# Attention heads in 32-row tiles of TensorE instead of block-diagonal operands, in a transformer layer with a mixture of experts

## The chip, the core and the metric

The kernel runs on one core of one Trainium2 chip. The metric is the device time of one execution in microseconds (us), the lower the better. The engines are TensorE (PE in the profile, its weight loads PEld), VectorE (DVE), ScalarE (ACT), GpSimd (POOL) and SyncE (SP, which here only issues DMAs). Each runs its own instructions in program order and waits on semaphores.

## The reference

One decoder layer on 16 sequences of 128 tokens of width 128, with a context of 77 tokens a sequence. Attention has 16 heads of width 8; the mixture of experts has 8 experts, of which each token uses 2. All is float32.

```python
def _attn(q_in, k_in, v_in, wq, bq, ..., causal):
    Q = (q_in @ wq + bq).reshape(Bq, Sq, H, HD)      # Kp and V in the same way
    scores = jnp.einsum('bqhd,bkhd->bhqk', Q, Kp) / jnp.sqrt(jnp.float32(HD))
    if causal: scores = jnp.where(mask, scores, -jnp.inf)
    a = jax.nn.softmax(scores, axis=-1)
    return jnp.einsum('bhqk,bkhd->bqhd', a, V).reshape(Bq, Sq, Dm) @ wo + bo

x = _layernorm(x + _attn(x, x, x, *sa, True), ln1_g, ln1_b)
x = _layernorm(x + _attn(x, encoder_output, encoder_output, *ca, False), ln2_g, ln2_b)
x = _layernorm(x + _moe(x, router_w, router_b, e_w1, e_b1, e_w2, e_b2), ln3_g, ln3_b)
```

## The kernel before

**Stages.** The attention part works on pairs of sequences: 8 pairs, `p`, and within a pair the sequence `u` (0 or 1). Each pair passes through self attention (SA), cross attention (CA) and the router (RT). The list `ORDER` (line 267) is the order of the steps in one iteration, written out by hand; a row `(SA, "scores", 2, 0)` is step, kind, part and how many pairs ahead or behind the iteration's own. Every engine walks through the same list and does its share of each step, so three pairs are under way at once, and an engine never takes a later step before an earlier one. Steps with four parts (`scores`, `weights`, `mix`, `restore`) have part = 2u + half, two groups of heads each. `home` (line 285) gives each step its PSUM banks. After the pairs comes the expert stage (39 slots of 128 rows, lines 603 to 628 on TensorE), and a last layer norm over all tokens (lines 996 to 1027), called the tail.

**Precision.** Queries and keys are split into a high and a low part in the reduced format fp32r. `spread_terms` multiplies them with the 0/1 matrices `spread` so that each head has 32 rows: 8 rows for the shift, and three times 8 for the products high x high, high x low, low x high. Four heads j = 0..3 fill the 128 rows of a group g = 0..3; the result is `qu` (by ScalarE, line 663) and `ku` (by VectorE, line 790), which also adds ones (`kones`) in the eight shift rows.

**Scores.** To keep the four heads of a group apart in one matmul over 128 rows, one operand is block-diagonal. `km` (line 503) has `ku`'s rows of head j in column block j and zeros elsewhere. GpSimd zeroes `km` and `qm` once (lines 1032 and 1033), and for each pair SP copies 24 rows of each head from `ku` to `km` (line 366, four DMAs) and from `qu` to `qm` (line 372, four DMAs). The scores of a group are one matmul of 512 columns (4 x 78 in CA), after a bf16 matmul with the causal mask in SA (line 502). VectorE takes the negated row maxima (`nm`, line 807), splits them (`mm`, lines 815 and 817), TensorE transposes them (line 510), and ScalarE writes them into the eight shift rows of each head in `qm`, in four copies (line 674):

```python
for j in range(J):
    rows = slice(32 * j, 32 * j + 8)
    src = bank[home[k, "shift", u][0]][rows, 0:P].rearrange("r (o n) -> r o n", o=1).to_broadcast([8, GROUPS, P])
    act.copy(k.qm[rows, :, j, P * u:P * u + P], src).then_inc(k.s_sha, 1)
```

**Weights, values, restore.** `weights` computes the shifted, transposed scores again as `ku` x `qm` (line 522), ScalarE takes the exponential into `pt` (line 682), and in SA GpSimd zeroes what lies over the diagonal (line 1048). `mix` multiplies a group's `vo` (32 value columns and 32 columns of ones, line 535) with 512 columns of `pt`; two groups stand in one bank, in rows 0 to 63 and 64 to 127. ScalarE copies the bank to `us` (line 689), `restore` transposes it back in four pieces (line 546), and VectorE takes the reciprocals of the sums and multiplies the head's own 8 of 32 value columns (lines 829 and 833). `turn_heads` and `norm` finish the attention: output projection, residual, batch-norm statistics (line 847), and on GpSimd the epsilon added to the variance (line 1056) and the power -1/2 (line 1058). The tail does the same at lines 1089 and 1091.

**Setup.** VectorE clears and fills constants (lines 757 to 772), counted in `s_setup`; the first `spread_terms` on TensorE and all of VectorE's steps wait for all of it. GpSimd adds the output bias to `residual` (line 1038) when that is loaded.

## Time and profile before

| | |
|---|---|
| median of 3 runs | 504.39 us (501.17 to 506.9) |
| the profiled execution | 503.74 us |
| its span (first to last instruction) | 501.9 us, 8915 instructions |
| TensorE busy, weight loads | 370.7 us (74%), 245.4 us (49%) |
| VectorE busy | 314.4 us (63%) |
| ScalarE busy | 283.2 us (56%) |
| GpSimd busy | 185.5 us (37%) |

The profile is of one execution. Busy time is the time in which an engine has an instruction under way; TensorE's matmuls overlap, and their ends are modelled, so the distance between starts says more than a duration. Idle time before an instruction is put down to what released it. In the span the first 60 us are the filling of the pipeline of pairs, 60 to 322 us its steady run, to 385 us its emptying and the router's last steps, to 470 us the experts, and then the tail.

### The profile page before, as it was taken

How to read it: one execution, taken by the hardware profiler on the slowest of the kernel's cores; microseconds unless marked ns; L12 is line 12 of the kernel's file. 1: busy time of each engine (PE TensorE's matmuls, PEld its weight loads, DVE VectorE, ACT ScalarE, POOL GpSimd, SP SyncE). 2: the span in 40 equal slices, each digit the busy share in tenths (PEclk: the TensorE clock that was granted, in tenths of full speed). 3: DMA queues.
4: the chain of work that ended last, by engine and by line, in shares of the span. 5: the costliest groups of instructions: out<-in, count | busy, mean ns of one | idle time of the engine just before them, and what ended most of it. 6: DMA issues, size and time to landing. Idle time of an engine off the chain costs nothing.

```text
span 501.9 us, 8915 instructions
## 1 busy us (share of the span) xinstructions
PE 370.7 (74%) x2121; PEld 245.4 (49%) x2121; DVE 314.4 (63%) x1055; ACT 283.2 (56%) x648; POOL 185.5 (37%) x253
## 2 busy tenths in 40 slices
PE   2348668989989989989988988757504999999300
PEld 1313445465455465455465463343203999999300
DVE  9632555678778778778778777455371555555192
ACT  2017268669669669679679669526211455555132
POOL 9403211231441441441441442512220455555363
PEclk9998899999999999999999999975855999999855
DMA  7330301511341341341341341040871122222243
GB/s 209 91 73 0 71 20 43 150 40 26 83 127 31 80 130 30 80 128 30 82 128 30 82 130 24 23 136 13 260 186 48 39 66 66 59 61 51 61 114 84
DMA packets 47819, 39.92 MB, mean 80 GB/s; under 512 B 4762, under 2 KB 44559, under 8 KB 47768
## 3 DMA queue, kind: packets, MB, share of 16 engines
q1 hardware_dynamic: 45496, 35.11, 27.3%
q0 software_dynamic: 2272, 4.24, 2.6%
q8 instruction: 20, 0.33, 0.3%
q14 instruction: 31, 0.25, 0.2%
HBM read 13.66 MB, written 14.79 MB: 57 GB/s over the span
## 4 chain that ended last, share of the span: by engine, by line
PE 26%; DVE 24%; issue 11%; POOL 10%; DVEq 7%; SPq 6%; ACT 6%; DMA 5%; POOLq 0%; ACTq 0%
POOL dispatched L1073 5%; PE bank L535 4%; SPq L366 4%; PE bank L479 4%; DVEq L977 3%; PE bank L522 3%; PE bank L480 3%; ACT ca_qm L674 2%; DVE ca_us L980 2%; DVE yb L990 2%; DVE ca_nm L807 2%; SPq L372 2%; PE bank L503 2%; DMA sa_km<-sa_ku 2%; DMA sa_xin<-in_x 2%
## 5 line engine op out<-in xcount | busy, mean ns | idle before, releaser
L733 ACT ACTIVATE sa_us<-bank,expert_b 128x128 f32<-128x128 f32 x156 | 45.0, 368 | 49.9 <-PE bank L617 38.5
L1048 POOL TENSOR_SCALAR_AFFINE_SELECT sa_pt<-sa_pt 128x512 f32<-128x512 f32 x64 | 39.1, 639 | 70.8 <-ACT sa_pt L682 70.7
L1082 POOL DMA_INDIRECT results<-sa_us,xs x39 | 41.6, 1066 | 52.9 <-DVE sa_us L992 50.3
L807 DVE TENSOR_REDUCE sa_nm<-bank 128x4 f32<-128x512 f32 x64 | 41.5, 684 | 14.0 <-PE bank L503 13.8
L1073 POOL DMA_INDIRECT dispatched<-r_sent,r_row x32 | 32.0, 1001 | 43.8 <-DVE r_sent L933 36.5
L617 PE MATMUL bank<-xsT,ca_us 128*128 128x128 f32 x312 | 45.8, 292 | 3.1 <-DVE ca_us L980 1.6
L674 ACT CAST sa_qm<-bank 8x512 fp32r<-8x512 f32 x64 | 36.9, 577 | 14.0 <-PE bank L510 12.3
L617 PEld LDWEIGHTS bank<-xsT,ca_us 128*128 128x128 f32 x312 | 39.7, 199 | 7.8 <-issue 4.6
L628 PE MATMUL bank<-ca_pt,sa_us 128*128 x312 | 42.3, 279 | 0.2 <-issue 0.2
L674 ACT CAST ca_qm<-bank 8x512 fp32r<-8x512 f32 x64 | 36.8, 576 | 9.0 <-PE bank L510 7.8
L682 ACT ACTIVATE sa_pt<-bank 128x512 f32<-128x512 f32 x64 | 34.8, 596 | 9.4 <-PE bank L522 9.3
L628 PEld LDWEIGHTS bank<-ca_pt,sa_us 128*128 128x128 f32 x312 | 38.6, 195 | 0.4 <-issue 0.4
L682 ACT ACTIVATE ca_pt<-bank 77x512 f32<-77x512 f32 x64 | 33.7, 598 | 9.0 <-PE bank L522 9.0
L503 PE MATMUL bank<-sa_km,sa_qu 128*128 128x512 f32 x64 | 37.5, 640 | 0.0
L502 PE MATMUL bank<-causal_bf,ident_bf 128*128 128x512 bf16 x64 | 27.1, 423 | 13.6 <-DMA sa_km<-sa_ku 12.8
L535 PE MATMUL bank<-ca_pt,ca_vo 77*64 77x512 f32 x128 | 35.8, 632 | 0.1
L535 PE MATMUL bank<-sa_pt,sa_vo 128*64 128x512 f32 x128 | 35.8, 631 | 0.0
L1056 POOL TENSOR_SCALAR sa_ve<-sa_ba 128x1 f32<-128x1 f32 x16 | 6.1, 384 | 69.1 <-DVE sa_ba L851 69.1
L807 DVE TENSOR_REDUCE ca_nm<-bank 128x4 f32<-128x308 f32 x64 | 26.8, 472 | 7.7 <-PE bank L503 7.4
L689 ACT COPY ca_us<-bank 128x512 f32<-128x512 f32 x32 | 18.8, 586 | 17.5 <-PE bank L535 16.9
L522 PE MATMUL bank<-sa_qm,sa_ku 128*128 128x512 f32 x64 | 24.3, 456 | 4.8 <-ACT sa_qm L674 3.6
L980 DVE COPY ca_us<-sa_pt 128x512 f32 x39 | 16.7, 427 | 15.2 <-PE bank L617 12.2
(207 smaller groups left out, 863.4 us busy)
## 6 DMA issues: line engine op xcount, KB each, us to landing
dispatched<-filler SPq DMA_DIRECT2D x17, 520.0 KB, 4.5
sa_km<-sa_ku SPq DMA_DIRECT2D x32, 96.0 KB
sa_qm<-sa_qu SPq DMA_DIRECT2D x32, 96.0 KB
ca_qm<-ca_qu SPq DMA_DIRECT2D x32, 96.0 KB
xs<-dispatched SPq DMA_DIRECT2D x39, 65.0 KB
sa_pt<-in_e_w SPq DMA_DIRECT2D x8, 256.0 KB, 5.0
ca_pt<-in_e_w SPq DMA_DIRECT2D x8, 256.0 KB, 6.1
sa_pt<-results SPq DMA_DIRECT2D x8, 256.0 KB, 4.9
```

Source lines behind the costliest of these rows:

```text
L503: pe.matmul(dst, k.qu[:, g, P * u:P * u + P], k.km[:, g, :, k.keys * u:k.keys * u + k.kpad], start=not k.causal, stop=True).then_inc(k.s_s ...
L522: pe.matmul(bank[b][0:k.keys, :], k.ku[:, g, k.keys * u:k.keys * u + k.keys], k.qm[:, g, :, P * u:P * u + P], start=True, stop=True).then_ ...
L535: ins = pe.matmul(bank[b][64 * (g % 2):64 * (g % 2) + 64, :], k.vo[:, u, g, :], k.pt[u][:, 512 * g:512 * g + 512], start=True, stop=True)
L617: ins = pe.matmul(bank[2 * b + c // 2][:, P * (c % 2):P * (c % 2) + P], w1_now[b][:, P * c:P * c + P], xsT[b][:, :], start=True, stop=True)
L628: ins = pe.matmul(bank[4 + b][:, 0:D], hid[b][:, c, :], w2[:, bass.ds(expert, 1), c, :].rearrange("f o d -> f (o d)"), start=(c == 0), sto ...
L674: act.copy(k.qm[rows, :, j, P * u:P * u + P], src).then_inc(k.s_sha, 1)
L682: act.activation(k.pt[u][:, 512 * g:512 * g + 512], bank[home[k, "weights", u][g % 2]][0:k.keys, :], ACT.Exp, scale=SCALE).then_inc(k.s_ex, 1)
L733: act.activation(hid[b][:, c, :], bank[2 * b + c // 2][:, P * (c % 2):P * (c % 2) + P], ACT.Gelu, bias=b1[:, bass.ds(expert * FC + c, 1)]) ...
L807: dve.tensor_reduce(k.nm[:, u, g, :], bank[home[k, "scores", u][g % 2]][:, :].rearrange("q (j n) -> q j n", j=J)[:, :, 0:k.keys], AX.X, AL ...
L1048: pool.affine_select(out=blockg, in_=blockg, compare_op=ALU.is_ge, fill=0.0, base=0, pattern=[[0, J], [1, P]], channel_multiplier=-1).then ...
L1073: pool.indirect_dma_start(out=dispatched, out_offset=bass.IndirectOffsetOnAxis(ap=r.row[:, v, c:c + 1], axis=0), in_=r.sent[:, v, c, :], i ...
L1082: pool.indirect_dma_start(out=results, out_offset=bass.IndirectOffsetOnAxis(ap=xs[v][:, P:P + 1].bitcast(I32), axis=0), in_=ys[v], in_offs ...
```

## The change

The block-diagonal operands `km` and `qm` go, with their memsets on GpSimd, their sixteen DMAs a pair on SP and the four copies of the shift on ScalarE.

- `scores`: each matmul takes the 32 rows of one head j of one group g from `qu` and `ku` (128 columns, 78 in CA). A part now holds two heads j (for all four g) in place of two groups; the matmuls of the two heads alternate and write different banks. The causal mask is put in the two banks first.
- `shift`: the transposed maxima are copied once, as `mT` (128x128).
- `weights`: for each g and each of the two heads one matmul `ku` x `qu` and one `pick` x `mT`, which adds the shift. `pick` is a new constant that selects the rows of group g. `ku` gets no ones any more, so a plain copy makes it.
- `mix`: one matmul for each head, over 128 columns and with 32 weight columns: 8 values, one column of ones, 23 zeros. The four groups stand in rows 0, 32, 64 and 96 of one bank, the heads j side by side. So one bank holds a whole sequence, `us` is copied once a sequence, and `restore` is done once, with four transposes.
- The epsilon goes into the statistics: a second, constant group of three numbers stands beside those of the row (`bs` has 9 columns instead of 6, of which the last is 128 epsilon), and GpSimd's addition goes. The tail does the same.
- `ys`, the experts' results, get tiles of their own, since `us` is half as large.

```diff
-            k.ku = t("ku", [P, GROUPS, 2 * keys], F32R)
-            k.qm = t("qm", [P, GROUPS, J, 2 * P], F32R)
-            k.km = t("km", [P, GROUPS, J, 2 * k.kpad], F32R)
-            k.vo = t("vo", [keys, 2, GROUPS, 64])
-            k.nm = t("nm", [P, 2, GROUPS, J])
+            k.ku = t("ku", [P, GROUPS, keys + k.kpad], F32R)
+            k.mT = t("mT", [P, 2, P], F32R)
+            k.vo = t("vo", [keys, 2, HEADS, 32])
+            k.nm = t("nm", [P, 2, J, GROUPS])
             k.mm = t("mm", [P, 2, J, 32], F32R)
             k.pt_all = t("pt", [P, 2 * GROUPS * 512])
             k.pt = [k.pt_all[0:keys, u * GROUPS * 512:(u + 1) * GROUPS * 512] for u in range(2)]
-            k.us = [t(f"us{u}", [P, 2, 512]) for u in range(2)]
-            k.rd = t("rd", [P, 2, 2, 2, J])
+            k.us = [t(f"us{u}", [P, 512]) for u in range(2)]
+            k.rd = t("rd", [P, 2, HEADS])
             k.on, k.oT, k.y, k.xn = (t(n, [P, 2, D]) for n in ("on", "oT", "y", "xn"))
-            k.bs, k.ba, k.ve, k.rs = t("bs", [P, 2, 6]), t("ba", [P, 2, 2]), t("ve", [P, 2]), t("rs", [P, 2])
+            k.bs, k.ba, k.ve, k.rs = t("bs", [P, 2, 9]), t("ba", [P, 2, 2]), t("ve", [P, 2]), t("rs", [P, 2])
...
-            (CA, "scores", 0, -1), (RT, "choose", 0, -2), (SA, "restore", 0, 0), (SA, "mix", 1, 0),
+            (CA, "scores", 0, -1), (RT, "choose", 0, -2), (SA, "mix", 1, 0),
...
-            def spread_terms(k, p, u):
-                if u == 0:
-                    return
-
-                if not after_pair(p):
-                    sp.wait_ge(k.s_zero, 2)
-                sp.wait_ge(k.s_ku, p * 2 + 2)
-                if after_pair(p):
-                    sp.wait_ge(k.s_s1_ps, p * 8)
-                for j in range(J):
-                    rows = slice(32 * j + 8, 32 * j + 32)
-                    sp.dma_start(k.km[rows, :, j, 0:2 * k.keys].bitcast(F32), k.ku[rows, :, :].bitcast(F32)).then_inc(k.s_bdk, 16)
-                sp.wait_ge(k.s_qu, p * 2 + 2)
-                if after_pair(p):
-                    sp.wait_ge(k.s_s2_ps, p * 8)
-                for j in range(J):
-                    rows = slice(32 * j + 8, 32 * j + 32)
-                    sp.dma_start(k.qm[rows, :, j, :].bitcast(F32), k.qu[rows, :, :].bitcast(F32)).then_inc(k.s_bdq, 16)
...
             def scores(k, p, part):
                 u, half = divmod(part, 2)
                 if part == 0:
-                    pe.wait_ge(k.s_bdk, p * 64 + 64)
                     pe.wait_ge(k.s_qu, p * 2 + 2)
-                for g in (2 * half, 2 * half + 1):
-                    b = home[k, "scores", u][g % 2]
+                    pe.wait_ge(k.s_ku, p * 2 + 2)
+                pair = (2 * half, 2 * half + 1)
+                for j in pair:
+                    b = home[k, "scores", u][j % 2]
                     take(b)
-                    dst = bank[b][:, :].rearrange("q (j n) -> q j n", j=J)[:, :, 0:k.kpad]
                     if k.causal:
-                        pe.matmul(dst, ident_bf[:, :], causal_bf[:, :].rearrange("q (o n) -> q o n", o=1).to_broadcast([P, J, P]), start=True, stop=False)
-                    pe.matmul(dst, k.qu[:, g, P * u:P * u + P], k.km[:, g, :, k.keys * u:k.keys * u + k.kpad],
-                              start=not k.causal, stop=True).then_inc(k.s_s1_ps, 1)
-                    give(b, k.s_nm, p * 8 + 4 * u + g + 1)
+                        pe.matmul(bank[b][:, :].rearrange("q (g n) -> q g n", g=GROUPS), ident_bf[:, :],
+                                  causal_bf[:, :].rearrange("q (o n) -> q o n", o=1).to_broadcast([P, GROUPS, P]), start=True, stop=False)
+                for g in range(GROUPS):
+                    for j in pair:
+                        b, rows = home[k, "scores", u][j % 2], slice(32 * j, 32 * j + 32)
+                        ins = pe.matmul(bank[b][:, P * g:P * g + k.kpad], k.qu[rows, g, P * u:P * u + P], k.ku[rows, g, k.keys * u:k.keys * u + k.kpad],
+                                        start=not k.causal, stop=not k.causal or g == GROUPS - 1)
+                        if g == GROUPS - 1:
+                            ins.then_inc(k.s_s1_ps, 1)
+                            give(b, k.s_nm, p * 8 + 4 * u + j + 1)
...
             def weights(k, p, part):
                 u, half = divmod(part, 2)
-                pe.wait_ge(k.s_sha, p * 8 + 4 * u + 4)
-                if part == 0:
-                    pe.wait_ge(k.s_bdq, p * 64 + 64)
-                    pe.wait_ge(k.s_ku, p * 2 + 2)
-                for g in (2 * half, 2 * half + 1):
-                    b = home[k, "weights", u][g % 2]
-                    take(b)
-                    pe.matmul(bank[b][0:k.keys, :], k.ku[:, g, k.keys * u:k.keys * u + k.keys], k.qm[:, g, :, P * u:P * u + P],
-                              start=True, stop=True).then_inc(k.s_s2_ps, 1)
-                    give(b, k.s_ex, p * 8 + 4 * u + g + 1)
+                pair = (2 * half, 2 * half + 1)
+                for j in pair:
+                    take(home[k, "weights", u][j % 2])
+                pe.wait_ge(k.s_sha, p * 2 + u + 1)
+                for g in range(GROUPS):
+                    for j in pair:
+                        b, rows = home[k, "weights", u][j % 2], slice(32 * j, 32 * j + 32)
+                        pe.matmul(bank[b][0:k.keys, P * g:P * g + P], k.ku[rows, g, k.keys * u:k.keys * u + k.keys], k.qu[rows, g, P * u:P * u + P],
+                                  start=True, stop=False)
+                    for j in pair:
+                        b, rows = home[k, "weights", u][j % 2], slice(32 * j, 32 * j + 32)
+                        ins = pe.matmul(bank[b][0:k.keys, P * g:P * g + P], pick[rows, g, 0:k.keys], k.mT[rows, u, :], start=False, stop=True)
+                        if g == GROUPS - 1:
+                            ins.then_inc(k.s_s2_ps, 1)
+                            give(b, k.s_ex, p * 8 + 4 * u + j + 1)
 
             def mix(k, p, part):
                 u, half = divmod(part, 2)
                 if part == 0:
                     pe.wait_ge(k.s_vo, p + 1)
-                for g in (2 * half, 2 * half + 1):
-                    b = home[k, "mix", u][g // 2]
-                    pe.wait_ge(k.s_pm if k.causal else k.s_ex, p * 8 + 4 * u + g + 1)
-                    if g % 2 == 0:
-                        take(b)
-                    ins = pe.matmul(bank[b][64 * (g % 2):64 * (g % 2) + 64, :], k.vo[:, u, g, :], k.pt[u][:, 512 * g:512 * g + 512], start=True, stop=True)
-                    if g % 2:
-                        ins.then_inc(k.s_u_ps, 1)
-                        give(b, k.s_us, p * 4 + 2 * u + g // 2 + 1)
+                b = home[k, "mix", u][0]
+                if half == 0:
+                    take(b)
+                for j in (2 * half, 2 * half + 1):
+                    pe.wait_ge(k.s_pm if k.causal else k.s_ex, p * 8 + 4 * u + j + 1)
+                    for g in range(GROUPS):
+                        ins = pe.matmul(bank[b][32 * g:32 * g + 32, P * j:P * j + P], k.vo[:, u, J * g + j, :],
+                                        k.pt[u][:, 512 * j + P * g:512 * j + P * g + P], start=True, stop=True)
+                ins.then_inc(k.s_u_ps, 1)
+                if half:
+                    give(b, k.s_us, p * 2 + u + 1)
 
             def restore(k, p, part):
-                u, h = divmod(part, 2)
-                b = home[k, "mix", u][h]
+                u = part // 2
+                b = home[k, "mix", u][1]
                 take(b)
-                pe.wait_ge(k.s_us, p * 4 + 2 * u + h + 1)
-                for j in range(J):
-                    ins = pe.transpose(bank[b][:, P * j:P * j + P], k.us[u][:, h, P * j:P * j + P], ident)
+                pe.wait_ge(k.s_us, p * 2 + u + 1)
+                for g in range(GROUPS):
+                    ins = pe.transpose(bank[b][:, P * g:P * g + P], k.us[u][:, P * g:P * g + P], ident)
                 ins.then_inc(k.s_t_ps, 1)
-                give(b, k.s_on, p * 4 + 2 * u + h + 1)
+                give(b, k.s_on, p * 2 + u + 1)
...
                 act.wait_ge(k.s_mt_ps, p * 2 + u + 1)
                 if after_pair(p):
                     act.wait_ge(k.s_s2_ps, (p - 1) * 8 + 4 * u + 4)
-                for j in range(J):
-                    rows = slice(32 * j, 32 * j + 8)
-                    src = bank[home[k, "shift", u][0]][rows, 0:P].rearrange("r (o n) -> r o n", o=1).to_broadcast([8, GROUPS, P])
-                    act.copy(k.qm[rows, :, j, P * u:P * u + P], src).then_inc(k.s_sha, 1)
+                act.copy(k.mT[:, u, :], bank[home[k, "shift", u][0]][:, 0:P]).then_inc(k.s_sha, 1)
...
-                u, h = divmod(part, 2)
-                act.wait_ge(k.s_u_ps, p * 4 + 2 * u + h + 1)
-                if after_pair(p):
-                    act.wait_ge(k.s_t_ps, (p - 1) * 4 + 2 * u + h + 1)
-                act.copy(k.us[u][:, h, :], bank[home[k, "mix", u][h]][:, :]).then_inc(k.s_us, 1)
+                u, half = divmod(part, 2)
+                if half == 0:
+                    return
+                act.wait_ge(k.s_u_ps, p * 4 + 2 * u + 2)
+                if after_pair(p):
+                    act.wait_ge(k.s_t_ps, (p - 1) * 2 + u + 1)
+                act.copy(k.us[u][:, :], bank[home[k, "mix", u][0]][:, :]).then_inc(k.s_us, 1)
...
-                setup(dve.memset(k.vo[:, :, :, 32:64], 1.0))
+                setup(dve.memset(k.vo[:, :, :, HD:HD + 1], 1.0))
+                setup(dve.memset(k.vo[:, :, :, HD + 1:], 0.0))
                 setup(dve.memset(k.mm[:, :, :, :].bitcast(F32), 0.0))
+                setup(dve.memset(k.ku[:, :, 2 * k.keys:].bitcast(F32), 0.0)) if k.kpad > k.keys else None
             setup(dve.memset(CA.hk[:, 2 * SC:].bitcast(F32), 0.0))
             setup(dve.memset(CA.lk[:, 2 * SC:].bitcast(F32), 0.0))
 
+            for stats in (SA.bs, CA.bs, bs3):
+                setup(dve.memset(stats[:, :, 6:8], 0.0))
+                setup(dve.memset(stats[:, :, 8:9], D * EPS))
...
+            setup(dve.tensor_copy(pick[:, :, :], kones.rearrange("r (g o) -> r g o", o=1).to_broadcast([P, GROUPS, P])))
...
-                    dve.wait_ge(k.s_bdk, p * 64)
                 n = 2 * k.keys
-                dve.tensor_tensor(k.ku[:, 2 * u:2 * u + 2, :], bank[home[k, "spread_terms", u][1]][:, :].rearrange("r (g n) -> r g n", g=2)[:, :, 0:n],
-                                  kones[:, 2 * u:2 * u + 2].rearrange("r (g o) -> r g o", o=1).to_broadcast([P, 2, n]), ALU.add).then_inc(k.s_ku, 1)
+                dve.tensor_copy(k.ku[:, 2 * u:2 * u + 2, 0:n], bank[home[k, "spread_terms", u][1]][:, :].rearrange("r (g n) -> r g n", g=2)[:, :, 0:n]).then_inc(k.s_ku, 1)
...
+                heads = bank[home[k, "mix", u][1]][:, :].rearrange("q (h r) -> q h r", h=HEADS)
+                dve.reciprocal(k.rd[:, u, :], heads[:, :, HD]).then_inc(k.s_rd, 1)
+                dve.wait_ge(k.s_rd, p * 2 + u + 1)
+                dve.tensor_tensor(k.on[:, u, :].rearrange("q (g j d) -> q j g d", g=GROUPS, j=J), heads[:, :, 0:HD].rearrange("q (j g) d -> q j g d", j=J),
+                                  k.rd[:, u, :].rearrange("q (j g o) -> q j g o", j=J, o=1).to_broadcast([P, J, GROUPS, HD]), ALU.mult).then_inc(k.s_on, 1)
...
-            for k in KINDS:
-                pool.memset(k.qm[:, :, :, :].bitcast(F32), 0.0).then_inc(k.s_zero, 1)
-                pool.memset(k.km[:, :, :, :].bitcast(F32), 0.0).then_inc(k.s_zero, 1)
...
-                pool.tensor_scalar(k.ve[:, u:u + 1], k.ba[:, u, 1:2], EPS, None, ALU.add).then_inc(k.s_ve, 1)
-                pool.wait_ge(k.s_ve, n)
-                pool.tensor_tensor(k.rs[:, u:u + 1], k.ve[:, u:u + 1], half[:, :], ALU.pow).then_inc(k.s_rs, 1)
+                pool.tensor_tensor(k.rs[:, u:u + 1], k.ba[:, u, 1:2], half[:, :], ALU.pow).then_inc(k.s_rs, 1)
```

TensorE's instructions in the middle of a steady iteration, from the router's step to the second cross shift. `sa_` and `ca_` are the self and the cross attention's tiles. Before:

```order
L575 MATMUL bank<-router_w,r_xT 128x8 x2
L535 MATMUL bank<-sa_pt,sa_vo 64x512 x2
L510 MATMUL bank<-cst,sa_mm 128x128
L503 MATMUL bank<-ca_km,ca_qu 128x4x78 x2
L546 MATMUL bank<-cst,sa_us 128x128 x4
L535 MATMUL bank<-sa_pt,sa_vo 64x512 x2
L503 MATMUL bank<-ca_km,ca_qu 128x4x78 x2
L522 MATMUL bank<-sa_qm,sa_ku 128x512 x2
L503 MATMUL bank<-ca_km,ca_qu 128x4x78 x2
```

After, in the same place (a row with x2 or x8 is so many matmuls):

```order
L566 MATMUL bank<-router_w,r_xT 128x8 x2
L525 MATMUL bank<-sa_pt,sa_vo 32x128 x8
L494 MATMUL bank<-cst,sa_mm 128x128
L485 MATMUL bank<-ca_ku,ca_qu 128x78 x8
L525 MATMUL bank<-sa_pt,sa_vo 32x128 x8
L485 MATMUL bank<-ca_ku,ca_qu 128x78 x8
L506 MATMUL bank<-sa_qu,sa_ku 128x128 x2
L510 MATMUL bank<-sa_mT,pick 128x128 x2
```

Two matmuls of 64x512 have become eight of 32x128, two of 128x4x78 eight of 128x78. The last two rows of after stand there four times one after the other, for the four groups, in place of the one row of line 522. The transposes of `sa_us` after the first half are gone; those after the second half stay.

ScalarE's instructions at the same place of the iteration. Before:

```order
L701 COPY r_xT<-bank 128x256
L705 COPY r_sent<-ca_x 128x4x128
L709 ACTIVATE r_by_expert<-r_by_expert 128x16
L689 COPY sa_us<-bank 128x512
L674 CAST sa_qm<-bank 8x4x128 x4
L689 COPY sa_us<-bank 128x512
L682 ACTIVATE sa_pt<-bank 128x512 x2
```

After:

```order
L688 COPY r_xT<-bank 128x256
L692 COPY r_sent<-ca_x 128x4x128
L696 ACTIVATE r_by_expert<-r_by_expert 128x16
L659 CAST sa_mT<-bank 128x128
L676 COPY sa_us<-bank 128x512
L667 ACTIVATE sa_pt<-bank 128x512 x2
```

The four copies into `sa_qm`, for which the next weights on TensorE wait, have become one into `sa_mT`, and of the two copies into `sa_us` one is left.

## Rows read from the trace of the kernel before

**Rows 1.** Busy time of each engine in five periods; the header names the columns.

```profile
core 0: us, PE busy (x) PEld busy (x) DVE busy (x) ACT busy (x) POOL busy (x), PEclk, DMA share, GB/s
97.50:285.00 187.50, 168.13 (x910) 99.23 (x908) 142.90 (x507) 141.95 (x295) 66.59 (x117) 1.00 0.31 78
```

**Rows 2.** PE's longest wait, 97.5 to 285 us: total, times, longest.

```profile
PE bank L502 <- DMA sa_km<-sa_ku: 3.4, 5, 1.0
```

**Rows 3.** Timeline of PE in one period: start us, us, engine, line, operation.

```profile
150.08 0.53 PE L503 MATMUL bank<-ca_km,ca_qu 128*128 128x312 f32 x2
150.44 0.60 PE L546 MATMUL bank<-cst,sa_us 128*128 128x128 f32 x4
...
150.77 0.27 PE L546 MATMUL bank<-cst,sa_us 128*128 128x128 f32 x1
...
150.97 0.65 PE L535 MATMUL bank<-sa_pt,sa_vo 128*64 128x512 f32 x2
150.97 0.20 PEld L535 LDWEIGHTS bank<-sa_pt,sa_vo 128*64 128x64 f32 x4 [0.17 <-issue]
...
151.45 0.60 PE L535 MATMUL bank<-sa_pt,sa_vo 128*64 128x512 f32 x2
151.98 0.56 PE L503 MATMUL bank<-ca_km,ca_qu 128*128 128x312 f32 x2
...
169.24 0.39 PE L502 MATMUL bank<-causal_bf,ident_bf 128*128 128x512 bf16 x1 [0.50 <-DMA sa_km<-sa_ku]
...
169.70 0.39 PE L502 MATMUL bank<-causal_bf,ident_bf 128*128 128x512 bf16 x1
```

**Rows 4.** Costliest groups, shapes apart: busy us, mean ns of one | idle before.

```profile
L535 PEld LDWEIGHTS bank<-sa_pt,sa_vo 128*64 128x64 f32 x128 | 7.1, 137 | 8.2 <-issue 7.4 <-POOL sa_pt L1048 0.7
L480 PEld LDWEIGHTS bank<-sa_lq,spread_lq 128*128 128x128 f32 x32 | 6.6, 207 | 0.0
L674 ACT CAST sa_qm<-bank 8x512 fp32r<-8x512 f32 x64 | 36.9, 577 | 14.0 <-PE bank L510 12.3
L689 ACT COPY sa_us<-bank 128x512 f32<-128x512 f32 x32 | 18.8, 588 | 4.9 <-PE bank L535 4.6
L1056 POOL TENSOR_SCALAR sa_ve<-sa_ba 128x1 f32<-128x1 f32 x16 | 6.1, 384 | 69.1 <-DVE sa_ba L851 69.1
```

**Rows 5.** Timeline of the start, and the landing time of `residual`'s load.

```profile
3.81 0.89 SPq L338 DMA_DIRECT2D residual<-in_x  x1
...
4.87 3.03 DVE L769 CAST spread_hq<-cst 128x128 fp32r<-128x128 f32 x2
...
10.43 0.47 ACT L656 ACTIVATE sa_hk<-bank,sa_square 128x256 fp32r<-128x256 f32 x1 [0.38 <-PE bank L466]
...
13.68 0.21 DVE L770 CAST ident_bf<-cst 128x128 bf16<-128x128 f32 x1
13.71 4.53 POOL L1038 TENSOR_TENSOR residual<-residual,sa_rows 128x2048 f32<-128x2048 f32 x1
13.81 4.51 DVE L771 CAST causal_bf<-cst 128x128 bf16<-128x128 f32 x1
...
19.19 0.55 PE L479 MATMUL bank<-sa_hq,spread_hq 128*128 128x256 f32 x1 [8.80 <-DVE sa_lq L781]
...
29.04 0.61 PE L502 MATMUL bank<-causal_bf,ident_bf 128*128 128x512 bf16 x1 [5.24 <-DMA sa_km<-sa_ku]
...
residual<-in_x SPq DMA_DIRECT2D x1, 0.5 KB, 9.7
```

**Rows 6.** The chain that ended last, in the last cross attention: start us, us.

```profile
330.35 0.81 SPq L366
...
332.85 2.27 DMA ca_km<-ca_ku
...
340.85 0.57 ACT ca_qm L674
```

**Rows 7.** The same chain in the tail.

```profile
484.73 1.25 POOL ve L1089
```

65 lines of the change are left out of this document (25 added, 40 removed).

## Prediction

> **What bounds the kernel now.** I read the busy time by stretch first, then what TensorE waits for, then its instructions in order of time, and last the chain of work at both ends of the program. From 97.5 to 285 us [rows 1] lie five periods of 37.5 us, one for each pair of sequences, all alike, with TensorE at full clock. In a period TensorE is busy 33.6 us (168.13/5), VectorE 28.6, ScalarE 28.4, GpSimd 13.3. All engines run the same written order, so a period is TensorE's 33.6 us and the 3.9 us in which it waits. The longest of these waits is the one for the copies that build `km`, 3.4 us in five periods [rows 2]; the rest are a dozen small ones. TensorE bounds the middle; a saving on ScalarE counts there only as far as TensorE waits for it. At both ends nothing is full, and each link of the chain counts whole.
>
> **TensorE's prices** [rows 3]. Per record (a matmul with its weights; a plain fp32 matmul is two records):
> - 512 columns: 0.23 us (bf16 mask and fp32r product together, 169.24 to 169.70: 0.46). A record of 128 columns and 128 weight columns: 0.11 (150.44 to 150.77, three steps).
> - Two column tiles run side by side: the 64-wide value products start in twos (150.97), the next two 0.48 later, the next block 0.53 after those. So 4 records of 512 fp32 columns cost 1.01 us, and four weight loads were through in 0.20 us.
> - Another tiling costs 0.09: the step from 150.77 to 150.97 is 0.20 and not 0.11; after the block 0.53 stands where 0.43 to 0.48 would, about 0.1. So 0.19 for going in and out.
> - Weight loads: 64 columns 137 ns, 128 columns 207 ns [rows 4], so some 70 ns for each 64, and between loads that follow each other 0.11 a load.
>
> **The middle, per period** (8 blocks of each kind: 4 self, 4 cross; one block is half of a sequence's heads).
> - Scores, self: before 8 x 0.46 = 3.7. After, a block is two masks (0.46), then 8 records of 32 rows and 128 columns in 4 side-by-side pairs. Such a record is not in the trace. Its ends: a pair could take 0.06 (128 columns at the rate of 512) or, with nothing beside anything and at the fp32 rate (0.43 for a record of 512, two records a matmul, so 0.21 for 128 columns), 0.43. I take 0.12 a pair: bound by one weight load of 128 columns, the nearest row, with the other row group's load beside it as with the column tiles. 0.46 + 4 x 0.12 + 0.19 = 1.13, x4 = 4.5: +0.8.
> - Scores, cross: before 8 x 0.18 (150.08 to 150.44 is two) and some start-up, 1.8. After 4 x (0.48 + 0.19) = 2.7: +0.9.
> - Weights, self: before two records of 512 and a start-up of 0.1, 0.57 a block, 2.3. After, 16 records (8 with `ku`, 8 with `pick`), 8 pairs: 0.96 + 0.19 = 1.15, x4 = 4.6: +2.3. Cross, with 77 weight columns, 0.08 a pair (77/64 of 70 ns): 4 x (0.64 + 0.19) = 3.3: +1.0.
> - Value products: before 8 x (1.01, which holds the way out, + 0.09 for the way in) = 8.8. After, a block is two heads' columns of 8 records, 128 columns each, in four column tiles: two passes of 0.11 side by side, 0.23 for 8 records, 2 x 0.23 + 0.19 = 0.65, x8 = 5.2: -3.6. Ends: this, or all records alone at 0.11, (16 x 0.11 + 0.19) x 8 = 15.6.
> - Restore: 8 blocks of four transposes (0.44) become 4: -1.8.
> Sum: +0.8 +0.9 +2.3 +1.0 -3.6 -1.8 = -0.4. TensorE has nearly as much work as before, 33.2.
>
> Around it: ScalarE loses 16 copies to `qm` at 577 ns, gets 4 copies of 128x128 at about 0.28 (an estimate, half of the 588 ns for four times the columns), and halves the 8 copies to `us` (588 ns) [rows 4]: 9.2 - 1.1 + 2.4 = 10.5 us less of 28.4. VectorE's restores halve, about -1.3. GpSimd loses 4 additions of 384 ns [rows 4]. None bounds the middle, so of this only TensorE's waits are paid back: the 3.4/5 = 0.7 for `km` go wholly, and of the rest about as much again (the input tile that queued on SP behind eight copies, `qm`, shorter norms). 3.9 goes to some 2.6. A period loses 0.4 + 1.3 = 1.7. GpSimd's four indirect stores stay, with VectorE queued behind them. Some seven periods (five alike, and the ramps beside them): **-12 us**.
>
> **The start** [rows 5]. VectorE's casts run slowly exactly while GpSimd works on SBUF: `ident_bf` took 0.21 us at 13.68, and `causal_bf`, the same size, 4.51 us beside GpSimd's 4.53 us addition. The four memsets of `qm` and `km` ran on GpSimd from the start, the first casts at 4.87 took 1.5 us each and more (two in 3.03), and TensorE waited to 19.19 for that setup. With the memsets gone GpSimd's addition still waits for `residual`, which is issued at 3.81 and lands 9.7 us later, so the casts have SBUF to themselves: nine casts at 0.21 and `pick` at about 0.6 instead of 13.6 us (4.87 to 18.45); the memsets that are added cost some 1.5 back. Setup is over by 9 and `lk` (from `hk`, 10.43 + 0.47) by 11.5: -7.6. Then the 5.2 us wait for the copies is gone: first scores at 16 and not 29.0, **-13 us**. In the first pair's own chain two rows of four `qm` copies (2.4 us each) become one, less the cold-clock cost of more records: **-3 us**.
>
> **The end.** In the last cross attention the chain goes through `km`'s copies (330.35 to 335.17, 4.8 us), `qm`'s (340.85 to 343.24, 2.1 more than a `mT` copy) [rows 6], two norms with an addition of 0.4 each, and a second restore: **-8 us**. In the last layer norm the addition (1.25 us) leaves GpSimd's chain [rows 7]: **-1.5 us**. The expert stage is untouched.
>
> Sum: -12 - 13 - 3 - 8 - 1.5 = -37.5. The profiled execution took 503.74 (span 501.9, 1.8 around it), 0.1% under the median of 504.39. 503.7 - 37.5 = **466 us**.
>
> A rule speaks against the change: the Trainium skill, TensorEngine Tiling (Array Packing), Key Properties, says that changing the tiling mode drains TensorE. The trace agrees with 0.09 us each way, so the 16 extra blocks of another tiling cost 16 x 0.19 = 3 us a period, which the sums above hold.
>
> **Rivals.**
> - A, row groups don't run beside each other (place: the 8-record and 16-record blocks of scores and weights; price: 0.11 a record instead of a pair). For: the trace shows no row tile; its 128-wide weight loads come 0.11 apart at best. Against: column tiles' loads did overlap. Extra: 16 self-score, 16 cross-score and 32 self-weight pairs x 0.12 and 32 cross-weight pairs x 0.08 = 10.2 us; TensorE goes to 43.4, the waits to 1.5, the period to 44.9, +7.4 x 7 = +52. With the ends' -25.5: about **530**. It decides from 5.3 us extra a period (5.3 - 1.7 = 3.6, x7 = 25). The same time comes if the pairs run beside each other but a 128-column fp32r record goes at the fp32 rate (0.21 a pair).
> - B, only two of the four column tiles overlap: 0.44 instead of 0.23 for 8 records, +0.21 x 16 = 3.4 a period, 3.4 - 1.7 = +1.7, x7 = +12: **490**.
> - C, records have a pace of their own of 0.11, whatever the tile: A's 10.2 and the value products at 15.6 instead of 5.2, 20.6 - 1.7 = +19 a period: **610**. For: no stretch of the trace keeps a faster pace. Against: two records started together at 150.97. The Trainium skill, TensorE: Matmul & The Clock Gate, Back-to-back issue gap, gives about 81 ns for a matmul of 128 columns with its weights in a stream; by it 320 records would take 26 us against my 13.9 for scores, weights and values without masks and changes, +10 a period, and the time would be 551, an estimate from that page. No row here shows such a stream.
> - D, the middle gives back what the ends win: TensorE +5.3 a period, by pairs at 0.16 instead of 0.12 and 0.08: **503**.
>
> **Chances.** Forecast 0.50, B 0.12, A 0.25, C 0.08, D 0.05. Faster by over 1% is forecast and B: 0.62; within 1% is D: 0.05; slower A and C: 0.33. One per cent is about what a measurement of this kernel tells from no change. The likeliest case's own range is 450 (pairs at 0.06, waits mostly gone) to 485. The range 450 to 536 takes in B, D and A (530, and a little) and leaves out C.
>
> **What would show it.** Right: first scores at about 16 us; periods near 36 us; a 16-record block of self weights in 1.1 us with starts in twos; 8 value records within 0.25 us; no wait on ScalarE before the weights. Wrong: starts 0.1 apart one by one in those blocks, periods over 40 with TensorE never waiting (A or C), value blocks over 1 us (B), or casts still over 2 us before the first scores.

## The result, and the profile after

| | before | after |
|---|---|---|
| median | 503.52 us (501.17 to 506.9, 4 runs) | 539.32 us (537.83 to 542.19, 4 runs) |
| ratio to before | | 1.071 (95% interval 1.063 to 1.079) |
| span of the profiled execution | 501.9 us | 540.5 us |

The change makes the kernel 7.1% slower. Forecast were 466 us, and the range of 450 to 536 missed the time as well. The head of the page of after (instructions, busy time, and TensorE's granted clock in tenths for 40 slices of the span) shows what changed most:

```profile
span 540.5 us, 12285 instructions
PE 436.1 (81%) x4041; PEld 351.8 (65%) x4041; DVE 293.0 (54%) x1001; ACT 205.6 (38%) x520; POOL 159.9 (30%) x213
PEclk9657559958757765975877677566555599999955
```

TensorE's busy time rose by 65 us, and that of every other engine fell. The clock row is where to look for the reason. The same row of before is:

```profile
PEclk9998899999999999999999999975855999999855
```

Before, the steady run stood at full clock [rows 1]; now it hardly reaches it.

The span can be cut at the same points of the program in both traces: the first scores, the projections of the second, fourth and eighth pair, the last scores, the first output of the experts (429.8 us in after, 388.2 in before) and the last (508.8 and 468.7). TensorE's busy time and granted clock in these stretches, of after:

```profile
14.50:36.60 22.10, 18.68 (x144) 0.57 0.13 43
36.60:118.70 82.10, 75.71 (x693) 0.69 0.06 18
118.70:299.30 180.60, 165.69 (x1690) 0.72 0.12 36
299.30:381.00 81.70, 69.36 (x673) 0.65 0.11 35
381.00:429.80 48.80, 21.00 (x180) 0.50 0.43 129
```

and of before (the columns are stretch, its length, busy us and instructions, clock, share and GB/s of the DMA engines):

```profile
29.00:47.80 18.80, 14.58 (x45) 0.82 0.11 26
47.80:118.90 71.10, 57.87 (x309) 0.98 0.26 62
118.90:269.10 150.20, 134.81 (x730) 1.00 0.31 80
269.10:340.90 71.80, 56.35 (x296) 0.94 0.26 69
340.90:388.20 47.30, 20.81 (x80) 0.61 0.46 133
```

The difference of the spans adds up from them: first scores 14.5 us earlier; then +3.3 to the second pair's projection, +11.0 to the fourth's, +30.4 in the four alike periods from there (45.15 us each, before 37.55), +9.9 to the last scores, +1.5 to the experts, -1.5 in the experts and -1.5 in the tail. -14.5 + 3.3 + 11.0 + 30.4 + 9.9 + 1.5 - 1.5 - 1.5 = +38.6 = 540.5 - 501.9.

In the four periods TensorE is busy 165.69 / 4 = 41.4 us each at a mean clock of 0.72. The product, 29.8 us, is its work at full clock; before it is 134.81 / 4 x 1.00 = 33.7. So the work fell, by 3.9 us a period, while the time rose by 7.6. (Such products of two means are good to some 2%.)

The timeline of TensorE in after (start, us until the last of the group ends, instructions; answers to [rows 3]). First rows in a stretch at full clock, a block of self weights, a block of cross weights and one of the value products:

```profile
147.15 0.33 PE L506 MATMUL bank<-sa_qu,sa_ku 32*128 32x128 f32 x2
147.31 0.27 PE L510 MATMUL bank<-sa_mT,pick 32*128 32x128 f32 x2
...
148.19 0.60 PE L480 MATMUL bank<-causal_bf,ident_bf 128*128 128x512 bf16 x2
...
167.73 0.28 PE L506 MATMUL bank<-ca_qu,ca_ku 32*77 32x128 f32 x2
...
168.42 0.64 PE L525 MATMUL bank<-sa_pt,sa_vo 128*32 128x128 f32 x16
169.00 0.33 PE L544 MATMUL bank<-cst,sa_on 128*128 128x128 f32 x1
```

then the same forms at half clock:

```profile
160.66 0.47 PE L506 MATMUL bank<-sa_qu,sa_ku 32*128 32x128 f32 x2
...
162.56 0.47 PE L494 MATMUL bank<-cst,ca_mm 128*128 128x128 f32 x1
162.97 1.07 PE L485 MATMUL bank<-ca_ku,ca_qu 32*128 32x78 f32 x8
```

The reader is to see two things. The records start in twos, 0.11 us after the last two (147.31, 147.42, 147.54, ...), so two row tiles do run side by side: a block of 16 records takes 148.19 - 147.15 = 1.04 us, the cross weights 168.42 - 167.73 = 0.69, and 16 value records 0.58. And at half clock these steps all but double: 0.21 between twos, 1.90 us for the block that begins at 160.66 (to 162.56), 1.0 for 8 cross-score records.

The largest wait of TensorE from 118.7 to 299.3 (answers to [rows 2]; in the four periods it idles 14.9 us in all, 3.7 each, where before idled 3.9):

```profile
PE bank L480 <- DVE sa_nm L798: 5.0, 8, 1.1
```

Nothing waits for copies of `km` or `qm` any more. In the start (answers to [rows 5]) VectorE's ten casts stand between 6.07 us and the end of this last one, and TensorE's first mask starts at 14.53:

```profile
7.49 0.22 DVE L765 CAST triangle_bf<-cst 128x128 bf16<-128x128 f32 x1
```

### The profile page after: what moved, and what is told of

Same layout as the page of the kernel before. It is cut to its first block, busy times and chain, and to the rows that moved or that the text cites. A ratio compares the mean times of both kernels' runs of the same rounds, so it can differ in the third digit from the quotient of the medians.

```text
span 540.5 us, 12285 instructions
## 1 busy us (share of the span) xinstructions
PE 436.1 (81%) x4041; PEld 351.8 (65%) x4041; DVE 293.0 (54%) x1001; ACT 205.6 (38%) x520; POOL 159.9 (30%) x213
## 4 chain that ended last, share of the span: by engine, by line
PE 52%; DVE 20%; issue 10%; DVEq 6%; ACT 3%; POOL 3%; DMA 3%; another core or an unknown queue 1%; SPq 1%; POOLq 0%; ACTq 0%
PE bank L485 7%; PE bank L506 7%; PE bank L525 6%; PE bank L510 5%; PE bank L457 4%; PE bank L458 4%; DVEq L963 3%; PE bank L537 3%; PE bank L480 2%; PE bank L438 2%; DVE sa_nm L798 2%; DVE ca_us L966 2%; DVE yb L976 2%; PE bank L494 2%; PE bank L550 2%
## 5 line engine op out<-in xcount | busy, mean ns | idle before, releaser
L1063 POOL DMA_INDIRECT results<-ys,xs x39 | 41.1, 1054 | 52.0 <-DVE ys L978 50.8
L506 PE MATMUL bank<-sa_qu,sa_ku 32*128 32x128 f32 x256 | 46.4, 369 | 1.5 <-ACT sa_pt L667 1.0
L510 PE MATMUL bank<-sa_mT,pick 32*128 32x128 f32 x256 | 45.1, 358 | 0.0
L1054 POOL DMA_INDIRECT dispatched<-r_sent,r_row x32 | 31.9, 996 | 42.7 <-DVE r_sent L919 35.4
L619 PE MATMUL bank<-ca_pt,sa_us 128*128 x312 | 43.9, 284 | 0.1
L506 PEld LDWEIGHTS bank<-sa_qu,sa_ku 32*128 32x128 f32 x256 | 36.5, 269 | 6.4 <-ACT sa_pt L667 4.7
L510 PEld LDWEIGHTS bank<-sa_mT,pick 32*128 32x128 f32 x256 | 37.3, 275 | 0.0
L485 PEld LDWEIGHTS bank<-ca_ku,ca_qu 32*128 32x128 f32 x256 | 28.7, 311 | 8.2 <-DVE ca_nm L798 4.9
L485 PE MATMUL bank<-ca_ku,ca_qu 32*128 32x78 f32 x256 | 32.3, 401 | 1.8 <-DVE ca_nm L798 1.1
L1039 POOL TENSOR_TENSOR sa_rs<-sa_ba,half 128x1 f32<-128x1 f32 x16 | 10.1, 634 | 78.5 <-DVE sa_ba L837 78.5
L525 PE MATMUL bank<-sa_pt,sa_vo 128*32 128x128 f32 x512 | 32.3, 399 | 0.0
L485 PEld LDWEIGHTS bank<-sa_ku,sa_qu 32*128 32x128 f32 x256 | 19.7, 216 | 15.1 <-issue 15.1
```

Of the source, the lines that this page charges most:

```text
L485: ins = pe.matmul(bank[b][:, P * g:P * g + k.kpad], k.qu[rows, g, P * u:P * u + P], k.ku[rows, g, k.keys * u:k.keys * u + k.kpad], start=n ...
L506: pe.matmul(bank[b][0:k.keys, P * g:P * g + P], k.ku[rows, g, k.keys * u:k.keys * u + k.keys], k.qu[rows, g, P * u:P * u + P], start=True, ...
L510: ins = pe.matmul(bank[b][0:k.keys, P * g:P * g + P], pick[rows, g, 0:k.keys], k.mT[rows, u, :], start=False, stop=True)
L525: ins = pe.matmul(bank[b][32 * g:32 * g + 32, P * j:P * j + P], k.vo[:, u, J * g + j, :], k.pt[u][:, 512 * j + P * g:512 * j + P * g + P], ...
L619: ins = pe.matmul(bank[4 + b][:, 0:D], hid[b][:, c, :], w2[:, bass.ds(expert, 1), c, :].rearrange("f o d -> f (o d)"), start=(c == 0), sto ...
L1063: pool.indirect_dma_start(out=results, out_offset=bass.IndirectOffsetOnAxis(ap=xs[v][:, P:P + 1].bitcast(I32), axis=0), in_=ys[v], in_offs ...
```

## The experiments

Four theories stood open. T1: tiles of 32 rows make TensorE lose its granted clock. T2: the clock follows how little TensorE has to do. T3: the trouble lies in the many short instructions, whatever their rows. T4: TensorE did not bound the middle of the kernel before, so that a saving there could bring nothing. The table gathers the steady periods of all runs of the whole kernel. Each is measured between the fourth and the eighth pair's projection and divided by four; "at full clock" is busy x clock.

| run | median us | ratio to before, 95% | period | TensorE busy | clock | at full clock |
|---|---|---|---|---|---|---|
| before | 503.6 | | 37.55 | 33.7 | 1.00 | 33.7 |
| after | 539.3 | 1.063 to 1.079 | 45.15 | 41.4 | 0.72 | 29.8 |
| e1 values alone | 503.3 | 0.997 to 1.005 | 37.5 | 30.6 | 0.93 | 28.4 |
| e2 tiles alone | 544.1 | 1.071 to 1.084 | 44.45 | 42.9 | 0.84 | 36.1 |
| e3 after and a fill | 548.6 | 1.085 to 1.092 | 46.55 | 43.9 | 0.85 | 37.4 |
| e4 after, shift full | 531.0 | 1.050 to 1.058 | 42.6 | 39.8 | 0.84 | 33.4 |
| e5 tiled scores | 515.6 | 1.017 to 1.032 | 41.8 | 37.5 | 0.78 | 29.2 |
| e6 tiled weights | 528.3 | 1.046 to 1.062 | 42.6 | 38.8 | 0.78 | 30.2 |
| e7 all rows | 573.4 | 1.133 to 1.151 | 48.55 | 46.1 | 0.83 | 38.3 |
| e9 values, start | 488.6 | 0.967 to 0.975 | 36.8 | 30.1 | 0.94 | 28.3 |
| e10 two queues | 494.3 | 0.979 to 0.987 | 36.35 | 30.0 | 0.95 | 28.5 |
| e11 shift apart | 477.8 | 0.945 to 0.952 | 36.65 | 31.8 | 0.99 | 31.5 |

### e1, e2: the two halves of the change

e1 is before with the value products per head and one restore a sequence, the rest as it was:

```diff
-                    ins = pe.matmul(bank[b][64 * (g % 2):64 * (g % 2) + 64, :], k.vo[:, u, g, :], k.pt[u][:, 512 * g:512 * g + 512], start=True, stop=True)
...
+                    for j in range(J):
+                        ins = pe.matmul(bank[b][32 * j:32 * j + 32, P * g:P * g + P], k.vo[:, u, J * g + j, :],
+                                        k.pt[u][:, 512 * g + P * j:512 * g + P * j + P], start=True, stop=True)
```

> The kernel before with only the value products changed: per head, 32 weight columns, 128 columns of pt, four column tiles, one copy and one restore a sequence; scores and weights stay block-diagonal. Theory 1 (the row tiles of scores and weights let TensorE's clock fall): the granted clock stays near 0.91, a period falls from 37.5 to 32 to 34 us by the 5.4 us taken from TensorE, time 465 to 480 us. Theory 2 (the short value records of 128 columns let the clock fall, or cost more than forecast): clock under 0.85, a period of 37 or more, time 500 or more.

e2 is after with before's `mix` and `restore` (the diff of e1 in reverse on after):

> The kernel before with scores, weights, shift and epsilon as in the changed kernel, but with the value products as before (64 wide, 512 columns, two banks, four restores). Theory 1 (row tiles lower the clock): clock at 0.75 or less, and TensorE's work at full clock some 5 us a period over before, so a period of 45 to 52 us and 540 to 590 us. Theory 2 (value records lower it): clock over 0.85, a period near 41, 495 to 510 us.

Measured: 503.3 and 544.1 us. Neither theory's numbers came whole. e1 has no row tile, yet its time and its period are those of theory 2, and over the whole span its clock stood at 0.85; but its value products did not cost more than forecast: TensorE's work at full clock fell by 5.3 us a period (forecast 5.4). e2's time is that of theory 1, with a clock of 0.84 in the periods that is above what theory 1 said.

What became of e1's 5.3 us: as the clock stood at 0.93 and not at 1.00, TensorE's busy time fell by 3.1 us a period only, and its idle time rose by 3.0, from 3.9 to 6.9. The period did not move. The waits of e1, in four periods from 116.9 us, show where the idle time went, the first above all:

```profile
PE bank L502 <- DMA sa_km<-sa_ku: 8.4, 4, 2.3
```

Before, this wait took 2.9 us in four periods. The next largest, for the maxima of the self attention, grew from 1.4 to 5.7. So T4 holds as far as this: before's middle was not bound by TensorE alone; 3.1 us less of its busy time became waits. These waits cost clock too. One of those for `km` lies in the first of the next two stretches of e1, and the masks and scores behind it, all over 128 rows, ran at about half clock:

```profile
126.90:129.40 2.50, 0.24 (x12) 1.00 0.45 98
129.40:131.90 2.50, 2.44 (x6) 0.53 0.56 119
```

The whole loss of the change is in e2, the tiles of the scores and weights with the shift that belongs to them.

### e3, e4: fill the array

e3 adds to after 24 full bf16 products a period, ahead of the tiles in their own banks:

```diff
                 for j in pair:
-                    take(home[k, "weights", u][j % 2])
+                    b = home[k, "weights", u][j % 2]
+                    take(b)
+                    pe.matmul(bank[b][:, :].rearrange("q (g n) -> q g n", g=GROUPS), ident_bf[:, :],
+                              causal_bf[:, :].rearrange("q (o n) -> q o n", o=1).to_broadcast([P, GROUPS, P]), start=True, stop=True)
```

(and the same in the cross scores; what it writes is overwritten).

> The changed kernel with 24 more bf16 matmuls of 128x128x512 a period, written into the banks ahead of the cross scores and of all weights and overwritten there: 24 x 0.213 = 5.1 us more work for TensorE at full clock, nothing less. Theory 1 (the whole loss is the half clock, which full-array work lifts): clock 0.85 or more, a period of 38 to 41 us, 490 to 515 us, faster than the changed kernel although it does more. Theory 2 (the records' own cost is the loss): TensorE's added work comes on top, a period of 50 and 575 us or more.

e4 replaces the four `pick` records of a bank by one product over 128 rows and 512 columns, and the one copy of the maxima by four masked ones:

```diff
+                for j in pair:
+                    pe.matmul(bank[home[k, "weights", u][j % 2]][0:k.keys, :], pick[:, j, 0:k.keys], k.mT[:, u].rearrange("r g n -> r (g n)"), start=True, stop=False)
...
-                    for j in pair:
-                        b, rows = home[k, "weights", u][j % 2], slice(32 * j, 32 * j + 32)
-                        ins = pe.matmul(bank[b][0:k.keys, P * g:P * g + P], pick[rows, g, 0:k.keys], k.mT[rows, u, :], start=False, stop=True)
```

> The changed kernel with the shift added by one matmul over all 128 rows and 512 columns for each bank (mT copied four times with the group's 0/1 column as scale) in place of four 32-row records: 64 tile records a period fewer, 16 full records of 512 columns more, about the same work at full clock (per block 4 x 0.12 + 2 x 0.22 = 0.92 instead of 0.96). Theory 1: the clock rises to 0.80 to 0.90 and the time falls to 490 to 515 us. Theory 2 (records' own cost): within 10 us of the changed kernel's 539.

Measured: 548.6 and 531.0 us. By the times neither of theory 1's ranges came, and e4's is within the 10 us of theory 2; by the clock theory 1 was right in both: it rose from 0.72 to 0.85 and 0.84. e4 had 3.6 us more full-clock work a period than after, where about the same was expected, and was still faster, by 8 us. It has 64 row-tile records a period fewer as well as 16 full products more, so it does not tell which of the two lifted the clock; e3, which only adds full products, shows that these alone do. In e3 the 24 products cost (37.4 - 29.8) / 24 = 0.32 us each, more than their own 0.21 (probably by changes of tiling beside them; this was not taken apart), and this ate the gain.

### e5, e6: one of the two kinds of tiles

e5 is e1 with tiled scores (without `km`) and block-diagonal weights; e6 is after with before's scores and `km`. Neither has an edit that is not shown above or in the change.

> Only the scores go by 32-row tiles (km, its copies on SP and its memset are gone); the weights stay block-diagonal over 128 rows, with qm, its copies on SP and on ScalarE; the value products are per head, as in e1. Two theories on which part of the change lowers the granted clock. By the share of row tiles: a third of after's row-tile records are left (16 pairs of 48 in self attention), the clock in the middle stands at 0.85 to 0.92, TensorE's 30 us of full-clock work take some 34, the wait for km (8.4 us in four periods in e1) is gone, the period is 36 to 38 and the time 490 to 505. By any run of row tiles, however short: clock 0.75 as in after, 30 / 0.75 = 40, period 43, 525 to 535. If the first holds the kernel also has most of the gain at the start (first scores at about 20 us).

> The reverse of e5: the scores stay block-diagonal over 128 rows (km, its memsets and its copies on SP as before), the weights go by 32-row tiles with pick records and one copy of the shift, as in after; value products per head, epsilon in the statistics. Two thirds of after's row-tile records are left. By the share of row tiles: clock 0.78 to 0.85 in the middle, TensorE's 30 us of full-clock work take 37, with km's wait the period is 40 to 42 and the time 515 to 530. If the weights with their 32 records a sequence half are what lowers the clock: 0.75, 535 to 540, and e5 is then near 490. If the scores are: 0.95 and 490 to 500, and e5 is then near 530.

Measured: 515.6 and 528.3 us, the clock 0.78 in both. The share of tiles was a bad guide: a third of them lowered the clock as much as two thirds. e5 fell between its two expectations (490 to 505 and 525 to 535), e6 into its first (515 to 530). e5's clock was expected at 0.85 to 0.92 by the share of tiles, so T1 in its simplest form, so much clock for so many tiles, fell here.

### e7: the same records over all rows

```diff
-                        b, rows = home[k, "scores", u][j % 2], slice(32 * j, 32 * j + 32)
+                        b, rows = home[k, "scores", u][j % 2], slice(0, P)
```

and so in the weights, with a `pick` whose other rows are zero. Each head gets the sum of its group's four scores, so the softmax is another one.

> After with the same number of records, of the same 128 columns and in the same order, but each over all 128 rows in place of 32 (scores and weights: each head is given the sum of the four heads of its group, in the scores as in the weights; pick has zeros in the rows of the other heads). No row tile is left; the records can't start in pairs, so TensorE's work at full clock rises by some 10 us a period (80 second records of pairs at 0.11 to 0.12), from 29 to 39. If it is the row tiles, of which two keep half of the array's rows idle, that lower the granted clock, it stands over 0.95 in the middle, the period is 41 to 43 and the time 505 to 525: faster than after with more work. If short records, each with its own weights, or a TensorE with little work lower it whatever their rows: 0.75, 39 / 0.75 = 52 and some waits, 580 to 590.

Measured: 573.4 us. The work at full clock rose to 38.3 as expected (39), but the clock stood at 0.83 and neither side's number came. These stretches show where it goes:

```profile
165.00:170.00 5.00, 4.33 (x40) 1.00 0.01 2
170.00:175.00 5.00, 4.47 (x47) 0.67 0.02 5
175.00:180.00 5.00, 5.00 (x26) 0.50 0.00 0
```

The clock falls among the first cross scores, whose records have 78 columns (8 of them at 171.29, 8 more at 173.77), and it had stood at 1.00 through the self scores and weights just before, whose full records have 128. TensorE also idled 0.67 and 0.53 us shortly before. So full rows alone don't suffice in the kernel, and the question became one of forms, each without a wait.

### e8, e12: each form by itself

Behind the last expert TensorE alone runs streams of one form, none of which waits for anything, each behind 72 full bf16 products. The kernel's outputs are those of after. Each of the two kernels ran once; the stream of pairs stands in e8 twice. In short:

```diff
+            def rows_of(heads, count):
+                for n in range(count):
+                    for j in heads:
+                        rows, g = slice(32 * j, 32 * j + 32), n % GROUPS
+                        pe.matmul(bank[j][:, P * g:P * g + P], SA.qu[rows, g, 0:P], SA.ku[rows, g, 0:P], start=True, stop=True)
+            full()
+            rows_of((0, 1), 260)
+            full()
+            rows_of((0,), 260)
...
```

> After, and behind its last expert TensorE alone runs streams of one record form each, with no wait between them, each behind 72 bf16 products of 512 columns over the full array (15 us): pairs of 32-row tiles (fp32r, 128 columns), one row tile at a time, four row tiles in turn, four 32-column tiles (fp32, 128 columns), full 128-row records of 128 columns (fp32r), the same with 512 columns, and pairs again. The full-array streams stand at clock 1.0 throughout. By the theory that tiles lower the clock with no wait in between: the pairs and the single tiles start at 1.0 and fall to 0.5 within their stream; the four row tiles and four column tiles, which fill the array, stay at 1.0 or fall later; the full 128-column records stay. By the rival that the waits of the kernel, and not the tiles, lower it: 1.0 in every stream. The time itself is some 180 us longer than after's TensorE part and says nothing.

> As e8, with other streams on TensorE alone behind the last expert, each behind 72 full bf16 products: pairs of 64-row tiles (128 columns), three 32-row tiles in turn, full 128-row records of only 78 columns, pairs of 32-row tiles of 78 columns, one full product and four pairs in turn, one full product and eight tiles in four row groups in turn, single 32-column tiles (fp32, 128 columns), and before's form of the value products (two 64-column tiles, 512 columns). Theory: a stream keeps the clock when the tiles under way together take up all of the array, and loses it when half or more of it stays empty. Pairs of 64 rows, the two 64-column tiles and the mixed stream with four row groups keep it; pairs of 32-row tiles of 78 columns, the single column tile and most likely the 78-column records lose it within 5 us by the steps between starts; three tiles and the mixed stream with pairs are open. Rival: 32-row tiles as such lose it, unless four run: then three tiles lose it and the 78-column full records keep it. The time says nothing.

The stretches of e8, TensorE's busy time (count) and granted clock. First the pairs of 32-row tiles (513.6 to 565.6), then single ones (from 582.8) and four in turn (653.7); the pairs come again from 832.8:

```profile
513.60:517.40 3.80, 3.75 (x68) 1.00 0.03 6
517.50:527.80 10.30, 10.30 (x102) 0.50 0.35 99
527.90:565.60 37.70, 37.70 (x358) 0.50 0.00 1
582.80:585.60 2.80, 2.73 (x24) 1.00 0.00 0
...
653.70:683.30 29.60, 29.55 (x1040) 1.00 0.02 4
```

The pairs lose the clock 3.8 us into their stream (5.4 the second time) and stay at half clock to its end, with TensorE busy 37.70 of 37.70 us; the single tiles lose it after 2.8 us; their steps go from 68 records in 3.8 us (0.112 us a pair) to 102 in 10.3 (0.20). Four row tiles in turn run at 1040 records in 29.6 us, 0.028 each, and keep the clock. So do four column tiles (699.0), full records of 128 columns (742.9) and full records of 512 (from 787.4 to 817.0 us, 130 records, clock 1.00):

```profile
699.00:727.50 28.50, 28.42 (x1040) 1.00 0.02 5
```

```profile
742.90:772.10 29.20, 29.14 (x260) 1.00 0.01 1
```

The stretches of e12: pairs of 64 rows (519.2); three 32-row tiles (549.5); full rows with 78 columns (589.3); pairs of 32 rows with 78 columns (629.4, at full clock for 3.6 us); one full product and four pairs in turn (671.0, at half clock from 677.4 to its end at 713.7); one full product and two rounds of four row groups (731.6):

```profile
519.20:533.70 14.50, 14.49 (x260) 1.00 0.27 75
549.50:554.50 5.00, 4.98 (x135) 1.00 0.02 3
554.60:572.60 18.00, 18.00 (x261) 0.50 0.01 2
589.30:595.40 6.10, 6.10 (x54) 1.00 0.01 3
595.60:611.40 15.80, 15.80 (x77) 0.50 0.00 0
633.20:653.70 20.50, 20.50 (x196) 0.50 0.01 2
671.00:677.40 6.40, 4.58 (x56) 1.00 0.00 0
731.60:759.40 27.80, 17.66 (x320) 1.00 0.01 2
```

and a single tile of 32 columns, fp32, and before's form of the value products:

```profile
775.00:803.50 28.50, 28.40 (x260) 1.00 0.00 1
```

```profile
819.20:875.00 55.80, 55.75 (x260) 1.00 0.00 1
```

The theory of e12, that the clock goes with an array half empty, fell on the single column tile, which uses a quarter of the columns and kept it. Its rival fell on the full records of 78 columns, which lost it. What sets the streams that lost the clock apart from those that kept it is this: those with tiles of 32 rows had fewer than four of them under way, and the one over all rows moved 78 columns in the step of 0.113 us (54 in 6.1 us) in which the full records of 128 that kept it moved 128. The single tile of 32 columns kept it with 77 rows, fewer than the 96 of three row tiles, which lost it; but it was fp32 and the row tiles fp32r, so neither what narrow weights do by themselves nor what a 32-row tile in fp32 would do is shown. Why in the chip this is so, no run shows.

T3 is excluded by the four row tiles, the shortest steps of all. T1 stands for these streams: one, two or three 32-row tiles at a time lost the clock without any wait, four did not. That full records of 78 columns lost it too says that 32-row tiles are not the only form that does. T2 is excluded as the only cause by the same streams, and stands as a second one: e1's clock fell behind a wait, and before itself, without any row tile, stood at 0.61 from 340.9 to 388.2 us, where TensorE was busy 20.81 us of 47.3. In the four periods, though, after idled no more than before (3.7 and 3.9 us each), at 0.72 against 1.00. The step from the streams to the kernel, whose blocks of tiles are about 1 us long with other products between them, is made by e2 and by the stream of one full product and four pairs, which lost the clock as well.

The Trainium skill, TensorE: Matmul & The Clock Gate, HAM oscillation — how this bites in real kernels, has it as the abstract rule that TensorE must not be left idle for long. e8 shows that this is not enough: 37.70 busy of 37.70 us at a clock of 0.50.

### e9, e10, e11: what is left of the change where the clock stays

e9 is e1 with the epsilon as in the change and another order of the start:

```diff
             for k in KINDS:
-                pool.memset(k.qm[:, :, :, :].bitcast(F32), 0.0).then_inc(k.s_zero, 1)
                 pool.memset(k.km[:, :, :, :].bitcast(F32), 0.0).then_inc(k.s_zero, 1)
+                if k.causal:
+                    pool.wait_ge(s_setup, SETUP)
+                pool.memset(k.qm[:, :, :, :].bitcast(F32), 0.0).then_inc(k.s_zero, 1)
```

> e1 (only the value products per head; weights and scores block-diagonal over 128 rows as before) with the two parts of the change that don't touch TensorE's rows: the epsilon in the statistics, and a start in which VectorE's casts don't run beside GpSimd's memsets (sa_km is zeroed first, the other three wait until VectorE's constants are done). Theory: the gains that the prediction gave to the start and the tail are real and add up where the clock stays. Casts at 0.22 us, constants done at about 8 us and not 18.5, first scores at 19 to 20 (29 less 9), the tail 1.5 and the norms of the last pairs some 1 us shorter: 503.3 - 9 - 1.5 - 1 = 492, 488 to 495. Rival: the loop through SP, or the first pair's own chain, takes the start's gain back: 500 to 503.

Measured: 488.6 us, within the range expected, at its low end. VectorE's last cast now ends at 7.4 us (`triangle_bf` at 7.15 + 0.22) and not at 18.45, the first scores come at 21.5 us and not at 29.0, and the tail takes 31.9 us (453.2 to 485.1) against 33.2. The first scores were expected at 19 to 20 us; the start gave 7.5 of the 15.4 us between the profiled spans of e1 and e9, the four periods 2.7 and the tail about 1. Where the other 4 lie was not followed up.

e10 issues two of `km`'s four copies from GpSimd:

```diff
+            def spread_terms(k, p, u):
+                if u == 0:
+                    return
+                pool.wait_ge(k.s_ku, p * 2 + 2)
+                if after_pair(p):
+                    pool.wait_ge(k.s_s1_ps, p * 8)
+                for j in (2, 3):
+                    rows = slice(32 * j + 8, 32 * j + 32)
+                    pool.dma_start(k.km[rows, :, j, 0:2 * k.keys].bitcast(F32), k.ku[rows, :, :].bitcast(F32)).then_inc(k.s_bdk2, 16)
```

> e9 with two of the four copies that build km issued by GpSimd in place of SP, at the same time as the other two. Theory: in e1 TensorE lost 5 us of work a period and the period stayed, because the middle is bound by a chain from ku over SP's copies to the scores and on; TensorE waited 8.4 us in four periods for km. With two queues the last copy lands 1.2 to 1.6 us earlier a pair: e9 less 8 x 1 to 1.5 = 480 to 485. Rival: another link (ScalarE's copies to qm, VectorE's maxima) bounds it, and km's wait only changes its name: within 0.5% of e9; or GpSimd's later steps (the masks of pt) are held up by the new issues: slower than e9 by up to 5 us.

Measured: 494.3 us, slower than e9 by 5.7. Its six executions lie between 488.3 and 497.3 us, and the profiled one is the fastest of them. In the steady periods of that one the wait for `km` fell from 8.5 to 6.7 us in four, the period by 0.45 us, and the waits for the maxima and for `ca_on` rose: the rival's "changes its name". What it lost lies in GpSimd's order at the start. Its copies stand behind the last of its start work and are issued at 21.2 us, where SP in e9 issues all four from 14.6 on:

```profile
16.79 4.49 POOL L1049 TENSOR_TENSOR residual<-residual,sa_rows 128x2048 f32<-128x2048 f32 x1
21.23 1.49 POOL L1059 DMA_DIRECT2D sa_km<-sa_ku  x2
```

so that the first scores came at 24.6 us, 3.1 later. The two profiled spans differ by 1.5 us. So the larger part of the 5.7 us between the medians lies in executions without a profile, and its cause is open.

e11 keeps e9's block-diagonal operands and takes the shift out of `qm`, over the full array:

```diff
                     pe.matmul(bank[b][0:k.keys, :], k.ku[:, g, k.keys * u:k.keys * u + k.keys], k.qm[:, g, :, P * u:P * u + P],
-                              start=True, stop=True).then_inc(k.s_s2_ps, 1)
+                              start=True, stop=False)
+                    pe.matmul(bank[b][0:k.keys, :], pick[:, g, 0:k.keys], k.md[:, u].rearrange("r j n -> r (j n)"),
+                              start=False, stop=True).then_inc(k.s_s2_ps, 1)
...
-                    src = bank[home[k, "shift", u][0]][rows, 0:P].rearrange("r (o n) -> r o n", o=1).to_broadcast([8, GROUPS, P])
-                    act.copy(k.qm[rows, :, j, P * u:P * u + P], src).then_inc(k.s_sha, 1)
+                    act.copy(k.md[rows, u, j, :], bank[home[k, "shift", u][0]][rows, 0:P]).then_inc(k.s_sha, 1)
```

(the experts' results and the tail's small statistics move into tiles that are free by then).

> e9 with the shift added as in the change, but over the full array: the maxima are copied once, block-diagonally (four copies of 8 x 128 by ScalarE, some 0.28 us each, in place of four of 8 x 512 at 0.58), and a product of pick, 128 rows, with 512 columns adds them in each bank of the weights. TensorE gets 16 products of 0.22 us more a period (3.5 us, it has 7 us of waits in e1), ScalarE loses 16 x 0.3 = 4.8 us, and the link from the maxima to the weights gets 1.2 us shorter. If ScalarE's link bounds the middle: 480 to 488; if not: within 1% of e9. The granted clock stays over 0.93 in the middle, since nothing is in row tiles and TensorE has more full-array work than in e1.

Measured: 477.8 us, 5.1% faster than before and faster than both kernels. The expected price came (four copies in 1.10 us against 2.38), but not the place: in the steady periods e11 gains next to nothing on e9 (36.65 against 36.8), with 3.2 us more work for TensorE in each. The time is under both ranges expected. The 7.7 us between the two spans are 1.0 at the first scores, 4.2 in the filling of the pipeline, 0.6 in the four periods, 3.1 from there to the experts, and 1.2 lost in the experts. TensorE by stretch, e11 from its first scores to its experts:

```profile
20.50:36.60 16.10, 14.41 (x72) 1.00 0.13 30
36.60:103.30 66.70, 54.62 (x453) 0.97 0.28 66
...
249.90:320.30 70.40, 53.83 (x460) 0.90 0.27 71
```

and e9 in the same:

```profile
21.50:40.00 18.50, 14.80 (x65) 0.60 0.07 17
40.00:108.50 68.50, 52.96 (x429) 0.93 0.27 64
...
255.70:327.20 71.50, 53.87 (x436) 0.80 0.26 70
```

In the second and third of these e11 has a higher clock with more instructions. The 1.00 of its first pair is not to be believed. Its products of 512 columns start there 0.42 to 0.43 us apart, which is half clock (at full clock it is 0.23), until 30.0 us:

```profile
28.27 0.63 PE L526 MATMUL bank<-sa_qm,sa_ku 128*128 128x512 f32 x1
28.69 0.63 PE L528 MATMUL bank<-sa_md,pick 128*128 128x512 f32 x1
...
30.71 0.40 PE L528 MATMUL bank<-sa_md,pick 128*128 128x512 f32 x1
30.94 0.40 PE L526 MATMUL bank<-sa_qm,sa_ku 128*128 128x512 f32 x1
```

So 9.5 of the 16.1 us ran at half clock, a mean near 0.70 against e9's 0.60 (an estimate from these steps). How much of the 7.7 us is the shorter link and how much the clock was not taken apart.

## Why the prediction was wrong

- **"With TensorE at full clock"** was read for the kernel before [rows 1] and then carried to the kernel after, in "TensorE's prices" and every term of the middle. This is the step that failed. The change takes away redundant work (block-diagonal operands, three quarters zeros) that had kept all rows in use, and the granted clock in the periods fell from 1.00 to 0.72. Only the first pair's term names a cold clock; in the middle, the end and every rival the clock of after is not an unknown. With 29.8 us of work at full clock and 3.7 us of waits a period would have been some 33.5 us (an estimate from these two) instead of 45.15. e8 shows the loss of clock by itself, e2 that it comes with the tiles of scores and weights, and e3 and e4 that full-array work lifts it again.
- **TensorE's prices** themselves were right at full clock, mostly a little high: a pair 0.112 us (forecast 0.12), the block of self weights 1.04 (1.15), of cross weights 0.69 (0.83), 16 value records with the way in and out 0.58 (0.65). The sum came to 29.8 us of work where 33.2 were forecast. The value products and restores took away 5.3 us (e1; forecast 5.4), while scores and weights together added 1.4 (after less e1; forecast 5.0); the prices above explain only a part of that difference, and the blocks of the cross scores were not seen at full clock in the rows read. Rivals B and C are refuted by the same rows: the value records run four at a time, and the row tiles in twos.
- **Rival A's 530** is near the time and its mechanism is absent. Its signs were to be "periods over 40 with TensorE never waiting" and starts one by one; the starts come in twos and TensorE waits 3.7 us a period. A period of 45.15 is what it forecast (44.9), which would have confirmed it for anyone who read only the totals.
- **"TensorE bounds the middle"** was also wrong (T4). The sum of its busy time and waits is a period for whatever engine one takes; e1 cut the busy time by 3.1 us and the waits grew by 3.0, and e11 added 3.2 us of work to e9 without a longer period. So it is doubtful that the -12 us forecast for the middle were to be had from TensorE's work even with the clock kept. What bounds the periods of 36.4 to 37.5 us in before, e1, e9, e10 and e11 stays open: the wait for `km` is the largest single one, but shortening it (e10) moved it to others.
- **The start**, -13: right, -14.5 at the first scores. e9 shows the same cause without any tile (casts of 0.22 us once GpSimd's memsets are out of their way, 7.5 us gained). **The first pair's chain**, -3: wrong in sign, +3.3. TensorE's busy time in it rose by 4.1 us at a clock of 0.57, and its idle time fell by 0.8.
- **The end**, -8: wrong, +9.9 to the last scores and +1.5 to the experts, at clocks of 0.65 and 0.50 (before 0.94 and 0.61). To the last scores TensorE's busy time rose by 13.0 us and its idle time fell by 3.1, so there the clock outweighed the links that are gone. In the stretch to the experts the busy time is the same (21.00 and 20.81) and the waits are 1.3 us longer; why is open.
- **The tail**, -1.5: right (31.7 against 33.2 us).

## What to carry to other kernels

Multiplying zeros is not only waste: here it held TensorE's clock. Before work is packed into small row tiles, price it at half clock too, and run the form by itself in a stream first; of the 32-row streams here only those with four row groups in turn, each in its own bank, kept the clock. And before an engine is called the bound, take work from it alone: here 3 us less of busy time a period (e1) brought nothing, while on top of that a start whose casts don't run beside memsets, one addition less in each norm, and the shift as a product over the full array brought 26 us.

## What the runs showed of the hardware

- Two 32-row tiles run side by side (0.112 us a pair of 128-column records, 0.20 after the fall), and four run in the time of one: 1040 records in 29.6 us. Whether four at a time keep the clock in the kernel was not tried: in e8 each row group writes a bank of its own, and the kernel's steps hold two. The Trainium skill, TensorEngine Tiling (Array Packing), Gotcha 1: PSUM Pressure, says that different row tiles can't use one bank at the same time; no run here shows it.
- The clock fell 2.8 to 6.4 us into the streams that lost it, and came back 3 us into the next full-array stream (the bf16 products after 565.87 stood at 0.50 until 568.6, then at 1.00).
- A round of one full product and four pairs took 0.913 us where 0.213 + 4 x 0.113 = 0.665 make up the work (7 rounds in 6.4 us): 0.25 for the two changes of tiling, where 0.19 was forecast.
- In the start the view can show a clock of 1.00 where the steps say half: the spreads of after's first pair start 0.21 us apart (10.30 to 10.51), later ones 0.12. The same holds for e11 up to 30.0 us, and for before up to about 31.8, so before's 0.82 from 29.0 to 47.8 is a little too high as well. There the distance between starts is what to go by.
- An idle TensorE loses clock too: e1, in which nothing runs in row tiles, stood at 0.53 for 2.5 us behind a wait of 2.3 us.
